# A layer of attention and a gated recurrence on one core: filler products, split weight parts and reordered loads in the prologue

## The reference

```python
xn = _layernorm(x, axis=-1)
x = x + _L0_attn_ref(xn, ...) + _L0_ffn_ref(xn, ...)

# attention: 16 heads of 64
qkv = data @ W_qkv + b_qkv
scores = jnp.einsum('nqhd,nkhd->nhqk', q, k)
attention = jax.nn.softmax(scores / jnp.sqrt(jnp.float32(HD)), axis=3)
out = jnp.einsum('nhql,nlhd->nqhd', attention, v).reshape(n, l, DIM)
return out @ W_out + b_out

# recurrence over the 8 sequences, as T = 8 steps with a batch of 512
def step(c, xt):
    ft = jax.nn.sigmoid(xt @ wf.T + c @ uf.T + bf)
    it = jax.nn.sigmoid(xt @ wi.T + c @ ui.T + bi)
    gt = jnp.tanh(xt @ wc.T + c @ uc.T + bc)
    return ft * c + it * gt, None
c_final, _ = lax.scan(step, c0, x)
h = jnp.tanh(jnp.einsum('tbi,oi->tbo', x, wo) + c_final @ uo.T + bo)
```

## Time and profile before

| | us |
|---|---|
| three runs: median (lowest to highest) | 830.48 (829.49 to 831.75) |
| profiled execution, time | 829.79 |
| its span | 828.0 |
| TensorE busy | 810.0 (98%) |
| GpSimd busy | 651.3 (79%) |
| VectorE busy | 546.9 (66%) |
| ScalarE busy | 481.0 (58%) |

### The profile page before, as it was taken

One profiled execution on the slowest core, in us unless ns is written; L12 is line 12 of the kernel. 1 busy time (PEld: TensorE's weight loads), 2 busy tenths in 40 slices (PEclk: granted clock), 3 DMA queues, 4 the chain that ended last, 5 costly groups with the idle time before them and its releaser, 6 DMA issues.

```text
span 828.0 us, 15510 instructions
## 1 busy us (share of the span) xinstructions
PE 810.0 (98%) x5397; PEld 476.9 (58%) x5397; DVE 546.9 (66%) x723; ACT 481.0 (58%) x638; POOL 651.3 (79%) x358
## 2 busy tenths in 40 slices
PE   5999999999999999999999999999999999999997
PEld 3656655675565655556555555557555555567543
DVE  6869666775776657665676657676576657676443
ACT  5746755664566636664666636665666636666450
POOL 4748799974787859887798859988698869988594
PEclk9999999999999999999999999999999999999999
DMA  9001010110001001010001000010001000031010
GB/s 279 2 28 52 3 54 27 39 42 13 16 26 41 12 17 15 14 28 26 1 14 39 1 26 13 1 39 26 1 14 39 1 26 12 3 78 15 2 27 13
DMA packets 62917, 23.31 MB, mean 28 GB/s; under 512 B 48386, under 2 KB 56608, under 8 KB 62880
## 3 DMA queue, kind: packets, MB, share of 16 engines
q1 hardware_dynamic: 62832, 22.81, 11.1%
q10 hardware_dynamic: 48, 0.02, 0.0%
HBM read 14.96 MB, written 6.55 MB: 26 GB/s over the span
## 4 chain that ended last, share of the span: by engine, by line
PE 91%; POOL 5%; DVE 1%; ACT 1%; issue 1%; DMA 1%; SPq 0%; POOLq 0%; DVEq 0%
PE st L958 20%; PE misc L972 14%; PE pv L972 13%; PE st L896 10%; PE mx L944 8%; PE st L964 6%; PE mx L1000 5%; PE st L991 4%; PE misc L879 3%; PE mx L879 3%; PE pv L896 2%; PE misc L896 2%; POOL PSUMK L387 1%; POOL PSUMK L394 1%; POOL PSUMK L381 1%; DVE NM L674 1%
## 5 line engine op out<-in xcount | busy, mean ns | idle before, releaser
L674 DVE TENSOR_REDUCE NM<-mx 128x2 f32<-128x1024 f32 x256 | 313.8, 1226 | 170.0 <-PE mx L944 170.0
L502 ACT ACTIVATE probs<-st 128x1024 f32<-128x1024 f32 x256 | 256.2, 1027 | 52.6 <-PE st L964 46.0
L381 POOL TENSOR_TENSOR PSUMK<-probs 128x1024 f32<-128x1024 f32 x64 | 154.1, 2408 | 36.8 <-ACT probs L502 36.8
L394 POOL TENSOR_TENSOR PSUMK<-PSUMK,probs 128x1024 f32<-128x1024 f32 x64 | 153.4, 2397 | 6.9 <-ACT probs L502 0.5
L387 POOL TENSOR_TENSOR PSUMK<-PSUMK,probs 128x1024 f32<-128x1024 f32 x64 | 153.1, 2393 | 6.6
L373 POOL TENSOR_TENSOR AL<-U,AH 128x512 fp32r<-128x512 f32 x60 | 77.1, 1288 | 81.5 <-ACT AH L494 81.5
L972 PE MATMUL misc<-probs,VALL 128*64 128x512 f32 x512 | 122.2, 598 | 0.0
L972 PE MATMUL pv<-probs,VALL 128*64 128x512 f32 x512 | 117.1, 599 | 0.0
L944 PE MATMUL mx<-KH,QH 64*128 64x512 f32 x512 | 107.2, 414 | 1.9 <-DVE NM L674 1.6
L958 PE MATMUL st<-QH,KH 64*128 64x512 f32 x512 | 103.9, 401 | 1.7 <-ACT probs L502 1.7
L958 PE MATMUL st<-QH,KL 64*128 64x512 f32 x512 | 101.4, 390 | 0.0
(11 more groups left out here) (194 smaller groups left out, 1304.9 us busy)
## 6 DMA issues: line engine op xcount, KB each, us to landing
MROW<-TT SPq DMA_DIRECT2D x256, 1.0 KB
x_store<-XH SPq DMA_DIRECT2D x8, 256.0 KB, 2.2
x_store<-XL SPq DMA_DIRECT2D x8, 256.0 KB, 2.4
RX<-R SPq DMA_DIRECT2D x124, 2.0 KB, 1.8
XSH<-x_store SPq DMA_DIRECT2D x7, 256.0 KB, 2.7
XSL<-x_store SPq DMA_DIRECT2D x7, 256.0 KB, 2.8
RES<-in_L_attn_data_dram SPq DMA_DIRECT2D x28, 64.0 KB, 2.9
out_dram<-RES SPq DMA_DIRECT2D x28, 64.0 KB, 1.9
```

The costliest lines, as they stand in the source:

```text
L381: nc.gpsimd.tensor_tensor(PSUMK[:, s % 2, :, :], e[:, :, 0, :], e[:, :, 1, :], ALU.add).then_inc(sum_part, 1)
L394: nc.gpsimd.tensor_tensor(PSUMK[:, s % 2, :, :], PSUMK[:, s % 2, :, :], probs[:, s % 2, :, 3, :], ALU.add).then_inc(sum_done, 1)
L502: nc.scalar.activation(probs[:, s % 2, :, u, :], st[:, u % 2, :, :], ACT.Exp, scale=SCALE).then_inc(exp_done, 1)
L674: nc.vector.tensor_reduce(NM[:, s % 2, 0:2 * TB].rearrange("p (h b) -> p h b", h=2)[:, :, b], mx[:, :, :], AX.X, ALU.max, negate=True).the ...
```

## The change

- TensorE multiplies the identity by itself 11 times before `turn_x(0)` and 5 times after the transpose of the biases, into the bank `mx[:, 1]`, which nobody reads before it is overwritten.
- Weights are rounded in five portions: the first 256 columns of q and of k (pairs 0 and 1), v, the other 768 of q, the other 768 of k. All low parts but k's first are GpSimd's. TensorE waits for the remaining portions (`wl_done[3]`, `wl_done[4]`) only ahead of pair 2.
- SyncE loads x of 1 and x of 2 apart, each behind a weight; the loads of x 3 to 7 move behind the transfers of the second maxima, the store of XH and XL behind those.
- `moments(1)` moves ahead of `lo_x(0)` on VectorE.
- ScalarE: the bias passes of pair 0 come before v's rounding, pair 1's after it; the rest of q and k is rounded behind `deviation(1, 3)`. Two of the four transfers of the first maxima are issued by ScalarE, behind the copies of `VALL`.
- TensorE: each `score_maxima` of pair 0 comes one place earlier, the fourth ahead of v's blocks 2 and 3; the wait for XSH moves to where it is read.

```diff
@@ loads (SyncE)
-            for i in range(2):
-                sp.dma_start(W_raw[:, i * DIM:(i + 1) * DIM], W_qkv[:, i * DIM:(i + 1) * DIM]).then_inc(ld_W[i], 16)
-            sp.dma_start(XN[:, 1:3, :, :], data_t[:, 1:3, :, :]).then_inc(ld_x[0], 16)
+            sp.dma_start(W_raw[:, 0:DIM], W_qkv[:, 0:DIM]).then_inc(ld_W[0], 16)
+            sp.dma_start(XN[:, 1, :, :], data_t[:, 1, :, :]).then_inc(ld_x[0], 16)
+            sp.dma_start(W_raw[:, DIM:2 * DIM], W_qkv[:, DIM:2 * DIM]).then_inc(ld_W[1], 16)
+            sp.dma_start(XN[:, 2, :, :], data_t[:, 2, :, :]).then_inc(ld_x[1], 16)
...
-            for n in range(3, N):
-                sp.dma_start(x_raw(n), data_t[:, n, :, :]).then_inc(ld_x[1 if n < 5 else 2], 16)
...
+            sp.wait_ge(pads_set, 4)
+            sp.wait_ge(tt_done, 1)
+            for g in range(2):
+                place_block(0, g)
+            place_max(1, 1)
+            for n in range(3, N):
+                sp.dma_start(x_raw(n), data_t[:, n, :, :]).then_inc(ld_x[2 if n < 5 else 3], 16)
             store_x(0)
-            sp.wait_ge(pads_set, 4)
-            place_max(0, 0)
-            place_max(1, 1)
@@ portions of the weights
+        PARTS = [slice(0, 2 * P), slice(DIM, DIM + 2 * P), slice(2 * DIM, 3 * DIM), slice(2 * P, DIM),
+                 slice(DIM + 2 * P, 2 * DIM)]
+        ROUNDED = (1, 2, 3, 4, 5)
@@ GpSimd
             lo_weights(0)
             lo_weights(2)
+            lo_weights(3)
+            lo_weights(4)
             standardise(1)
@@ ScalarE
             hi_weights(1)
+            act.wait_ge(bias_col, 1)
+            hi_q(0, 0, first_q[0])
+            hi_k(0, 0, first_k[0])
             hi_weights(2)
+            hi_q(1, 1, first_q[1])
+            hi_k(1, 1, first_k[1])
             hi_state(0)
-            for s in range(2):
-                hi_q(s, s, first_q[s])
-                hi_k(s, s, first_k[s])
             deviation(1, 3)
+            hi_weights(3)
+            hi_weights(4)
             for tb in range(TB):
                 evac_v(tb + 1, 0, tb, first_v[tb])
+            act.wait_ge(pads_set, 4)
+            act.wait_ge(tt_done, 1)
+            for g in range(2, 4):
+                to = MROW[0:HD + 1:HD, 0, 0, :].bitcast(f32).rearrange("p (b g i) -> p b g i", b=TB, g=4)
+                act.dma_start(to[:, :, g, :], TT[32 * g:32 * g + 2 * TB, 0, :]).then_inc(d_m[0], 16)
             for k in range(2):
                 hi_gates(k)
@@ VectorE
             standardise(0)
+            moments(1)
             lo_x(0)
             lo_weights(1)
...
-            moments(1)
             moments(2)
@@ TensorE
+            def keep_busy(count):
+
+                for i in range(count):
+                    nc.tensor.matmul(mx[:, 1, 0:P], ident[:, :], ident[:, :], start=True, stop=True)
+
+            keep_busy(11)
             turn_x(0)
             pe.wait_ge(ld_b, 16 * 7)
             nc.tensor.transpose(misc[:, 0:BIASES], brow[0:BIASES, :], ident[0:BIASES, 0:BIASES]).then_inc(bias_tr, 1)
+            keep_busy(5)
```

More of the change, by code:

```diff
@@ L253, in place_max, with place_block @@
                 sp.sem_inc(passed_sp, 1)
+                for g in range(4):
+                    place_block(s, g)
+            def place_block(s, g):
                 to = MROW[0:HD + 1:HD, s // 2 % 2, s % 2, :].bitcast(f32).rearrange("p (b g i) -> p b g i", b=TB, g=4)
-                for g in range(4):
-                    of = 32 * g
-                    sp.dma_start(to[:, :, g, :], TT[of:of + 2 * TB, s % 2, :]).then_inc(d_m[s % 2], 16)
+                sp.dma_start(to[:, :, g, :], TT[32 * g:32 * g + 2 * TB, s % 2, :]).then_inc(d_m[s % 2], 16)
             sp.wait_ge(xl_done, 1)
@@ L530, in _ @@
             act.wait_ge(bias_half, 1)
-            for i in range(3):
+            for i in range(5):
                 act.wait_ge(wl_done[i], 1)
@@ L594, in spread @@
             def spread(n, blocks=range(TB)):
-                dve.wait_ge(ld_x[(n - 1) // 2 if n < 5 else 2] if n else ld_x0, 16 if n < 3 else 32 if n < 5 else 48)
+                dve.wait_ge(ld_x[n - 1 if n < 3 else 2 if n < 5 else 3] if n else ld_x0, 16 if n < 3 else 32 if n < 5 else 48)
                 for b in blocks:
@@ L625, in lo_weights @@
             def lo_weights(i):
-                dve.wait_ge(wh_done, i + 1)
-                nc.vector.tensor_tensor(WL[:, i * DIM:(i + 1) * DIM], W_raw[:, i * DIM:(i + 1) * DIM],
-                                        WH[:, i * DIM:(i + 1) * DIM], ALU.subtract).then_inc(wl_done[i], 1)
+                dve.wait_ge(wh_done, ROUNDED[i])
+                nc.vector.tensor_tensor(WL[:, PARTS[i]], W_raw[:, PARTS[i]], WH[:, PARTS[i]],
+                                        ALU.subtract).then_inc(wl_done[i], 1)
             def lo_x(n):
@@ L1044, in _ @@
             project(0, 1, DIM, k_done, first_k[1])
+            score_maxima(0, 0, 1)
             pe.wait_ge(wl_done[2], 1)
@@ L1047, in _ @@
             project_v(0, 0, XH[:, 0, :], XL[:, 0, :], first_v[0])
[L1048 removed]
+            score_maxima(0, 0, 2)
             project_v(0, 1, XH[:, 0, :], XL[:, 0, :], first_v[1])
@@ L1052, in _ @@
             fold((0, 1))
-            score_maxima(0, 0, 2)
+            score_maxima(0, 0, 3)
             for tb in range(2, TB):
@@ L1090, in step @@
                         pe.wait_ge(gw_hi, 1)
+                        pe.wait_ge(wl_done[3], 1)
                         project(0, 2, 0, q_done, first_q[2])
@@ L1096, in step @@
                         pe.wait_ge(gw_hi, 2)
+                        pe.wait_ge(wl_done[4], 1)
                         project(0, 2, DIM, k_done, first_k[2])
@@ L1106, in step @@
                         pe.wait_ge(k_lo, 3)
+                        pe.wait_ge(d_xs, 32)
                         project_values(0, 0, (0, 1, 2), 64)
```

17 lines of the change are left out of this document (7 added, 10 removed).

## The result

| | before | after |
|---|---|---|
| median of 20 runs | 829.75 us (828.57 to 832.66) | 831.61 us (829.52 to 835.44) |
| profiled execution: time, span | 829.79, 828.0 | 833.09, 831.3 |
| mean granted clock of TensorE in it | 1.00 | 0.996 |
| last reduction of the start, maxima (3,3,3) | 45.64 | 49.05 |

Here (1,1,0) are the first maxima of pair 1 and (3,3,3) the fourth of pair 3; the reductions of the maxima mark how far the start has come.

What follows compares the result with a forecast made beforehand. TensorE bounds the unchanged body, so only the first 46 us count: 1.05 us earlier at maxima (1,1,0) less a 0.6 us load wait is 0.45, giving 829.3 profiled, 830.0 us median, range 828.2 to 832.0.

Steps and rivals of the forecast that it cites:

- Parts 1 and 2: Before the first maxima: identity products free, clock high from transposes, q0 at 8.9, first reduction at 11.8, 3.1 us earlier.
- Part 3: At v's projection: its late low part leaves 0.9 of 3.1 us; maxima (1,1,0) then come 1.05 us earlier.
- the sum: Whole kernel: profiled 829.79 us less 0.45 is 829.3; the median, 0.69 above the profiled run, is forecast at 830.0.
- rival B: Clock not high at q0, v late, maxima (1,1,0) 1.8 us late: slower, 832.8 us; chance 0.08.
- rival C: Clock rises late, in the five products after the bias transpose; gain only 0 to 0.1: 831.0 us; chance 0.10.
- Part 4: Two DMA issues on ScalarE ahead of the gate casts: 0.55 us each, no loss, first exp at 25.9.
- Part 5: Late loads of x 3 to 7: VectorE's moments(3) waits 0.6 us for x4, leaving 0.45 us at 46 us.
- rival A: At the late loads: x4 lands in time and the full 1.05 us stays: 829.4 us; chance 0.28.

Runs made afterwards that it cites:

- kernel 2: The changed kernel plus five more identity products ahead of TensorE's wait for v's low part, loads still late: 830.78 us, ratio 1.0003.
- kernel 12: A repeat of kernel 3, the changed kernel with early loads and five more identity products: 829.31 us, ratio 0.9989.
- kernel 3: The changed kernel with loads of x 3 to 7 early again and five more identity products ahead of v: 829.65 us, ratio 0.9993.
- 9: kernel 3 with all four transfers of the first maxima on SyncE, none on ScalarE: 828.97 us, ratio 0.9981.
- kernel 7: kernel 3 with v's blocks 2 and 3 ahead of the fourth maxima again: 829.52 us, ratio 0.9993.
- 11: kernel 6 with two of the four transfers of the first maxima put back on ScalarE: 828.08 us, ratio 0.9973.
- kernel 8: The kernel before with only its loads of x 3 to 7 moved behind the second maxima: 831.46 us, ratio 1.0024.
- Kernel 5: The changed kernel without its 11 and 5 identity products: 831.92 us, ratio 1.0030.
- kernel 6: From the kernel called 9: v's weights in two portions of 512 columns, rounding and v blocks reordered, two identity products ahead of the second maxima: 827.93 us, ratio 0.9973.
- kernel 4: The kernel before with the 11 and 5 identity products alone: 829.30 us, ratio 0.9991.
- kernel 1: The changed kernel with the loads of x 3 to 7 back behind W_out's load: 831.46 us, ratio 1.0017.

## Why the prediction was wrong

**Parts 1 and 2 held.** The identity was free, the clock high at the transposes and at q; q came at 9.20 for 8.9, the first reduction at 12.33 for 11.8. XH was 0.76 late, since x0 was there at 3.73 (3.39 before) and VectorE's standardising took 1.63 us for 1.11; the slack ahead of XL took up half of that.

**Part 3 named the hole and left out its price.** "TensorE idle for 1.3 us ahead of it" was 1.39, and `project_v(0)` came at 15.00 for 14.75. The step that failed is the one after: I had written "I take the clock as high from the transposes on" and never asked again, so the sum has no term for a clock that falls behind that hole, though rival B and rival C are about that clock, both only before 10 us. The low clock from 16.3 to 23 cost 2.3 us (24.65 against kernel 2's 22.02, less the 0.32 of its earlier start). Where the clock held, the term was right: 22.02, 22.04 and 22.08 in kernels 2, 12 and 3, for 21.8. The Trainium skill (TensorE: Matmul & The Clock Gate, The HAM clock gate) has the throttle as the resting state and activity as what lifts it; I used that rule for the start of the activity only. The traces show the way back too: a fall at 16.3 us, behind 1.39 us without work.

**Part 4 held.** The two issues took 1.21 us on ScalarE for 1.1 to 1.2, and cost nothing here: behind them and the Exp table QH, at 28.22, had still waited 1.09 us for TensorE, and kernels 12 and 9 have 22.78 and 22.79 to the last. In the orders of 7 and 11 they do cost.

**Part 5 was the right mechanism at too small a size.** x4 was to land 3.25 us after its issue (34.9 for 31.65); it took 3.46 to 4.13 in four executions. The wait was 0.78 to 1.47 instead of 0.6, and the loss to the last reduction 0.88 (8), 0.97 (5) and 1.62 (after). I chose near the lower end "since little else moves then". But x5 to x7 are issued right behind and share the way: the DMA issues after, 30 to 45 us, show 3.1 us for x3, 4.1 for x4 and 4.2 for x5 (KB each, us to landing):

```profile
OT<-in_L_attn_data_dram SPq DMA_DIRECT2D x1, 256.0 KB, 3.1
TG<-in_L_attn_data_dram SPq DMA_DIRECT2D x1, 256.0 KB, 4.1
RES<-in_L_attn_data_dram SPq DMA_DIRECT2D x1, 256.0 KB, 4.2
```

The window from the issue of x3 to the landing of x4 shows the sharing:

```profile
34.14:38.72 4.58, 4.58 (x35) 2.84 (x33) 2.80 (x4) 3.21 (x5) 4.42 (x2) 1.00 0.70 199
```

199 GB/s over 4.58 us are 0.91 MB, and x3 and x4 have 0.52, so 0.39 MB of what was issued behind x4 had moved before it was there. The same sum gives 0.18 MB in kernel 8, 0.29 in 5 and 0.32 in 2, in the order of x4's 3.46, 3.54 and 3.89 us.

The Trainium skill's fixed time plus bytes over 436 GB/s (DMA: Bandwidth & Descriptors, Anatomy of one DMA) gave 3.2 us for x3 and x4 together, 2.75 from x4's own issue; the measured 3.46 to 4.13 are above that, and rival A is out: VectorE waited in all four executions. Nor did I ask what TensorE's idle time behind that wait does to the clock (kernel 2, from 39.6).

**The sum.** Forecast at the last reduction: 0.45 earlier; measured 3.41 later. The 3.86 between them: 0.2 by v and the places behind it (22.0 for 21.8), 0.3 by the later start, 2.3 by the low clock, 1.0 by the loads. In medians it is less: the mean clock of the profiled execution, 0.996, is under that of the middle runs (0.997 and 0.998), and 7 of the 20 held it. Those 7 have a median of 829.94, within 0.1 of the 830.0 forecast, and this is partly luck, since the wait for x4 cost more than its 0.6 in every profile that has it. For the median over all runs the forecast lacked a term of 1.6 us.

Rival B's end, slower, came true by B's agent at another place: a clock that is low when v's blocks are projected, not when q's are. It had a chance of 0.08 because I looked for it only ahead of q.

## What to carry to other kernels

Where products without a purpose are put in to raise TensorE's clock, follow the clock on to the next place where TensorE waits: here 1.4 us of idle time was followed by 6.7 us of full work at 1.2 GHz in the profiled execution, and 13 of 20 runs had a low clock. Fill that hole as well, or cut the piece of work that makes it into portions no larger than the first consumer needs (v's low part in two halves, in kernel 6 together with a new order). A load that is moved from an idle time to just ahead of its use has to be priced with all loads issued behind it, and with what its consumer's idle time does to the clock. An issue on an engine that has slack in one order (ScalarE here and in kernel 12) can bind in the next (kernel 7).

## What the runs showed of the hardware

- **The clock fell behind idle times of 1.4 and 2.0 us, and in part of the executions only.** After the 1.39 us without work in 13 to 15 us of the profile after it fell at 16.3; after 2.04 us in kernel 2 at about 39.6. After 2.31 us at 38.7 to 41.05 in the profile after it stayed: the rows from 41 to 46 show 1.00. Kernel 5 has a hole as well (TensorE busy 0.49 in 15 to 16 us and 0.60 in 16 to 17) and kept the clock in its profile, and so did kernel 4 behind 1.01 us. So no single length of idle time decides in these runs. What does, the traces don't tell.
- **In the changed kernel the time of a run goes with its clock.** 829.52 us at 0.999, 835.44 at 0.992. Where all runs held the clock (7, 9, 11 and 12) they spread by 0.8 to 1.35 us. But the clock is not all of it: the kernel before held it in 103 of the 111 runs beside kernels 1 to 12, and these spread from 828.79 to 832.26.
- **The moment at which it rises varies too.** In the profile before it was high after 15 us, nine matmuls taking 4.18 us at the low level; in kernel 8, whose TensorE program up to there is the same, the pitch turns at 12.9 us, and the first reduction is at 14.15 for 14.88. With the identity ahead the transposes took 0.66 in the profile after, but 1.09, the low level, at 6.40 in kernel 12.
- **VectorE's standardising was stretched by GpSimd.** The four instructions take 1.63 us (after), 1.59 (5) and 1.52 (6) where GpSimd's low part of 256 columns, 0.7 to 0.8 us, starts 0.31 to 0.53 us into the group. In the profiles of the eight other kernels with that portion it starts 0.83 us into the group or later, and the four take 1.11 or 1.12. That is 0.4 to 0.5 us on the path to the transposes. The Trainium skill (SBUF — State Buffer, SBUF: two separate sides) says that VectorE, in certain of its instructions, and GpSimd share one port pair which one instruction holds alone. That GpSimd's starts inside the group, and the group is longer by less than GpSimd's instruction, agrees with it. The 0.5 us need not reach the end: in kernel 1, where the group took 1.11 and the transposes stood at 6.65 (7.14 after), `q` came at 9.18 all the same (9.20), since VectorE waited for x1 until 7.40 ahead of XL.

What stays open: what brings the clock down at one time and not at another, above all in kernel 3's profile, where no idle time over 0.50 us precedes it.
